# A 16-batch conv, attention and FFN kernel on one Trainium2 core: state blocks by head, z turned by DMA, other PSUM banks in the first phase

## The chip, the cores and the metric

The program runs on one core of one Trainium2 chip. The metric is the device time of one execution, in microseconds (us). Engines: PE (TensorE, the matrix engine; PEld are its weight loads), DVE (VectorE), ACT (ScalarE), POOL (GpSimd) and SP (SyncE, which here only issues DMAs; SPq is its DMA queue in the profile). Each engine runs its own instruction stream in order, and they meet only at semaphores.

## The reference, cut to what matters

x is 16 batches of 128 channels by 1024 positions. A channel mix by a 128x128 inverse gives t, 1024 tokens of 128 channels in each batch. Then

```python
t = t + attn(ln(t))          # causal linear attention, 8 heads of 16, feature map elu + 1
t = t + ffn(ln(t))           # gate averaged over the tokens picks W1, W2 of the batch
# attn: q, k, v = ln(t) @ W.T ; S = cumsum(k (x) v) ; z = cumsum(k)
#       out = (q @ S) / max(q . z, 1e-6) @ Wout.T
```

In the kernel most matrix operands are split into two f16 parts, hi and lo (lo = value - hi), and a product is made of two or three f16 matmuls.

## The kernel before

The first phase walks over 128 tiles (16 batches of 8 tiles of 128 tokens). For each tile the engines run named steps. TENSOR_ORDER, SCALAR_ORDER, VECTOR_ORDER, GPSIMD_ORDER and SYNC_ORDER give, for each engine, the steps in the order in which they are issued inside one **slot**, each with a skew: in slot s a step of skew k works on tile s - k. So one slot holds work on many tiles, and the time of the first phase is about 128 slots and a fill and a drain. The batches between the first and the last are a hardware loop with 8 slots in it; `batch` writes one batch out. Every step waits on semaphores for what it reads and for the buffer that it overwrites.

The steps, by tile: SP loads x; ACT `split_x` makes x_hi and POOL `split_x` makes x_lo (every second slot, two tiles at once); PE `conv` writes t into a bank of PSUM; DVE `stats1`, `mean_var1`, `eps1` and POOL `rsqrt1` (a power of one column) give 1/std; PE `project` writes q, k and v; ACT `exp_qk`, `relu_qk` and DVE `make_qk` (min(exp, 1) + relu) give q and k; `q_hi` (ACT), `k_hi` and `qk_lo` (POOL) split them into `qk_parts`; SP `turn` transposes that block by DMA into `qkT_parts`; ACT `v_hi` and DVE `v_lo` split v; PE `state` adds k (x) v to the running state in the bank `p_s`; PE `scores` writes a mask and k q into the banks `p_a`; ACT `scores_hi` and DVE `scores_lo` split them; PE `values` makes the numerators and denominators; DVE `denominator`, `invert`, `divide`; PE `turn_out`, ACT `copy_out`, PE `out_project` (which also adds the conv again), ACT `read_t1`; DVE `stats2`, `mean_var2`, `eps2`, POOL `rsqrt2`, DVE `normalise` give z = ln(t); z has to be turned and split for the gate (PE `gate`, ACT `gate_relu`) and for the second phase.

PSUM before: `p_in` has two banks (tiles of even and odd number), `p_a` one pair for the 1024 columns of the scores, `p_m1` one bank shared by `conv`, `out_project` and `gate`, `p_m2` one shared by `turn_out` and `turn_z`, and `p_o` and `p_s` one each. `bank_read` makes a step wait until the previous user of its bank has been read.

The state before is made for two heads at once, 128 rows of k parts by 2 x 17 columns, with 8 matmuls. The blocks across heads are of no use, so DVE `read_state` multiplies the bank by a mask into f32, and POOL `state_hi` and `state_lo` split it. z is turned by PE (`turn_z`) into `p_m2`, ACT `z_hi` and DVE `z_lo` split it from there.

Between the first batch and the loop SP sends the parts of the base FFN weights to memory and back (`base_parts`, then `W_hi_lo_rows`), and its later DMAs stand behind that.

The second phase (merged weights by batch, FFN, layer norm, store) begins when all gates are there and is not touched.

## Time and profile before

| | |
|---|---|
| median of 3 runs (lowest, highest) | 848.0 us (845.4, 848.01) |
| the profiled execution | 848.7 us |
| its span, first to last instruction | 846.9 us |
| busy share of the span: PE, PEld, DVE, ACT, POOL | 87%, 64%, 88%, 79%, 63% |
| mean granted PE clock, share of full speed | 0.969 |
| DMA | 74.10 MB, mean 87 GB/s |

Durations are those of the hardware profiler. Instructions of one engine overlap a little: the next one starts before the previous one's recorded end, so from one start to the next is often less than a duration. A matmul's recorded duration contains the way through the array and says little about how fast matmuls follow one another.

### The profile page before, as it was taken

The numbers are of one execution on the slowest core, as the hardware profiler recorded it, in microseconds if no ns is written. First come the engines' busy times: TensorE is split into PE (matmuls) and PEld (weight loads), VectorE is DVE, ScalarE is ACT, GpSimd is POOL, SyncE is SP. The second block draws the span as 40 slices with busy tenths as digits, with TensorE's granted clock in tenths as the row PEclk, the third lists the DMA queues.
The fourth block names the chain that finished last, engine by engine and source line by source line (L and its number), as shares of the span: only waits on it lengthen the run. The fifth ranks groups of instructions, "written<-read, shape, count | busy, mean of one in ns | idle before, by whom it ended". The sixth has DMA issues, their size and how long they took to land. (4 is left out here: it accounts for less than half of the span.)

```text
span 846.9 us, 37199 instructions
## 1 busy us (share of the span) xinstructions
PE 739.7 (87%) x11168; PEld 538.4 (64%) x11168; DVE 742.6 (88%) x2736; ACT 670.2 (79%) x1875; POOL 534.6 (63%) x1009
## 2 busy tenths in 40 slices
PE   1588999999999999999999999968899998899994
PEld 1255666666666666666666666648577777577773
DVE  6587999999999999999999999955788985689894
ACT  1477898999989989998898988844788885688884
POOL 5486888888888888888988988810133342033333
PEclk9888999999999999999999999977999999999998
DMA  2255444454444444544454444410022221122222
GB/s 80 52 126 118 98 111 105 92 117 109 91 111 106 105 105 100 116 106 99 106 111 95 116 100 98 88 33 26 2 77 86 77 74 51 38 64 76 74 87 75
DMA packets 165473, 74.10 MB, mean 87 GB/s; under 512 B 139212, under 2 KB 152687, under 8 KB 165368
## 3 DMA queue, kind: packets, MB, share of 16 engines
q1 hardware_dynamic: 165432, 73.58, 36.0%
q8 instruction: 23, 0.38, 0.2%
q14 instruction: 18, 0.15, 0.1%
HBM read 22.69 MB, written 17.30 MB: 47 GB/s over the span
## 5 line engine op out<-in xcount | busy, mean ns | idle before, releaser
L795 DVE SCALAR_TENSOR_TENSOR scores_lo<-p_a,scores_hi 128x512 f16<-128x512 f32 x256 | 164.0, 682 | 0.0
L698 ACT ACTIVATE scores_hi<-p_a 128x512 f16<-128x512 f32 x256 | 138.5, 600 | 6.4 <-PE p_a L543 6.2
L861 POOL TENSOR_TENSOR stats<-stats,consts 128x1 f32<-128x1 f32 x128 | 78.1, 610 | 75.7 <-DVE stats L745 75.6
L1312 POOL TENSOR_TENSOR ffn_rstd_shift<-ffn_rstd_shift,consts 128x4 f32<-128x4 f32 x32 | 36.7, 1146 | 132.8 <-DVE ffn_rstd_shift L1271 132.8
L886 POOL TENSOR_TENSOR qk_parts<-qk_f,qk_parts 128x128 f16<-128x128 f32 x256 | 104.9, 429 | 0.1
L867 POOL TENSOR_TENSOR stats<-stats,consts 128x1 f32<-128x1 f32 x128 | 89.0, 695 | 18.7 <-DVE stats L751 17.1
L560 PE MATMUL p_o<-v_parts,scores_hi 128*128 128x17 f16 x1024 | 90.2, 171 | 12.1 <-ACT scores_hi L698 6.2
L560 PEld LDWEIGHTS p_o<-v_parts,scores_hi 128*128 128x128 f16 x1024 | 80.4, 96 | 30.0 <-issue 27.6
L1095 PE MATMUL psb<-merged_W_of_batch,h_hi 128*128 128x128 f16 x512 | 94.2, 220 | 4.9 <-DVE h_lo L1249 3.8
L1249 DVE TENSOR_TENSOR h_lo<-h_f,h_hi 128x512 f16<-128x512 f32 x128 | 95.0, 782 | 1.2 <-ACT h_hi L1152 1.2
L1141 ACT ACTIVATE h_f<-psb,merged_b_of_batch 128x512 f32<-128x512 f32 x128 | 87.0, 711 | 11.4 <-PE psb L1076 11.3
L1097 PE MATMUL psb<-merged_W_of_batch,h_lo 128*128 128x128 f16 x512 | 93.8, 219 | 0.0
L1096 PE MATMUL psb<-merged_W_of_batch,h_hi 128*128 128x128 f16 x512 | 93.8, 219 | 0.0
L564 PE MATMUL p_o<-v_parts,scores_lo 128*128 128x17 f16 x1024 | 89.7, 170 | 0.0
L562 PE MATMUL p_o<-v_parts,scores_hi 128*128 128x16 f16 x1024 | 89.5, 170 | 0.0
L1161 ACT ACTIVATE normed<-psb,ffn_rstd_shift 128x128 f32<-128x128 f32 x128 | 48.1, 456 | 41.6 <-DVE ffn_rstd_shift L1277 41.6
L562 PEld LDWEIGHTS p_o<-v_parts,scores_hi 128*128 128x128 f16 x1024 | 80.3, 96 | 0.3 <-issue 0.2
L564 PEld LDWEIGHTS p_o<-v_parts,scores_lo 128*128 128x128 f16 x1024 | 80.0, 96 | 0.0
L768 DVE SCALAR_TENSOR_TENSOR qk_f<-exp_qk,relu_qk 128x256 f32<-128x256 f32 x128 | 75.3, 589 | 4.7 <-ACT exp_qk L666 3.4
L536 PE MATMUL p_a<-mask_bf,ident_bf 128*128 128x512 bf16 x256 | 78.1, 386 | 0.4 <-DVE scores_lo L795 0.4
L1305 POOL TENSOR_TENSOR normed<-normed,ln_gain_rows 128x512 f32<-128x512 f32 x32 | 40.7, 1272 | 58.5 <-ACT normed L1161 58.5
L650 ACT ACTIVATE t<-p_m 128x128 f32<-128x128 f32 x128 | 35.5, 277 | 47.7 <-PE p_m L589 45.5
(195 smaller groups left out, 3009.6 us busy)
## 6 DMA issues: line engine op xcount, KB each, us to landing
x_f<-in_x SPq DMA_DIRECT2D x32, 256.0 KB, 2.9
t_rows<-t SPq DMA_DIRECT2D x64, 128.0 KB, 1.9
t_back<-t_rows SPq DMA_DIRECT2D x32, 256.0 KB, 2.6
out<-out_tile SPq DMA_DIRECT2D x32, 256.0 KB, 2.0
tv_share<-in_L_ffn_tv_W SPq DMA_DIRECT2D x32, 128.0 KB, 2.2
qkT_parts<-qk_parts SPq DMA_TRANSPOSE x128, 3.1
...
```

Source lines behind the costliest of these rows:

```text
L560: mm(num[:, h, :], hi, vp[:, t, h, 0:VW], start=(h == 0), stop=False, skip_group_check=True)
L562: mm(num[:, h, 0:DH], hi, vp[:, t, h, VW:VW + DH], start=False, stop=False, skip_group_check=True)
L564: last = mm(num[:, h, :], lo, vp[:, t, h, 0:VW], start=False, stop=True, skip_group_check=True)
L698: nc.scalar.activation(ah[:, t % 2, cols], p_a[:, cols], ACT.Relu).then_inc(ahi_ready[eo], 1)
L795: nc.vector.scalar_tensor_tensor(al[:, t % 2, cols], p_a[:, cols], 0.0, ah[:, t % 2, cols], ALU.max, ALU.subtract).then_inc(alo_ready[eo], 1)
L867: nc.gpsimd.tensor_tensor(s[:, 8:9], s[:, 9:10], mhalf, ALU.pow).then_inc(rstd2, 1)
L886: last = nc.gpsimd.tensor_tensor(lo, src, pk[:, t % 4, w, :, 0:DH], ALU.subtract)
L1095: mm(o, hi, w2b[:, bb, 0, c, :], start=False, stop=False)
L1096: mm(o, hi, w2b[:, bb, 1, c, :], start=False, stop=False)
L1097: last = mm(o, lo, w2b[:, bb, 0, c, :], start=False, stop=(c == FC - 1))
L1141: nc.scalar.activation(hf_[:, c, :], ps[:, c, :], ACT.Relu, bias=b1s[:, h // 2, c:c + 1], scale=1.0 / WS).then_inc(h_ready[c], 1)
L1249: nc.vector.tensor_tensor(hl[:, h % 2, c, :], hf_[:, c, :], hh[:, h % 2, c, :], ALU.subtract)\
```

## The change

- **State by head.** PE `state` makes 16 matmuls of 64 weight columns by 17 or 16, each head into its own 64 partitions of `p_s`. DVE clears `p_s` once at the start, so that the blocks across heads stay zero. `read_state`, its f32 tile and the multiplication by ones are gone: ACT `state_hi` and DVE `state_lo` split the bank directly.
- **z by DMA.** `turn_z` on PE is gone. ACT `z_hi` and POOL `z_lo` split z before it is turned, and SP `turn_z` transposes both parts with one DMA into `zT_hi_lo`.
- **Banks.** `p_in` has one bank; `p_a` has two pairs; `conv`, `out_project`, `turn_out` and `gate` share `p_m1`.
- **Engines and order.** `q_hi` goes from ACT to POOL. All order tables and skews are other ones; the deepest skew is 12 where it was 8, so two batches are written out on either side of the loop.

```diff
-TENSOR_ORDER = [("conv", 0), ("project", 0), ("turn_out", 5), ("gate", 8), ("values", 4), ("turn_z", 7),
-                ("state", 2), ("out_project", 5), ("scores", 2)]
+TENSOR_ORDER = [("scores", 3), ("out_project", 6), ("values", 4), ("conv", 0), ("state", 2), ("turn_out", 5),
+                ("project", 0), ("gate", 11)]
...
-GPSIMD_ORDER = [("qk_lo", 2), ("state_lo", 4), ("split_x", 0), ("rsqrt2", 7), ("state_hi", 3), ("k_hi", 1),
-                ("rsqrt1", 0)]
-SYNC_ORDER = [("turn", 2), ("load_x", 3), ("load_tv", 3), ("store", 7)]
+GPSIMD_ORDER = [("rsqrt1", 1), ("rsqrt2", 8), ("split_x", 0), ("z_lo", 9), ("k_hi", 1), ("q_hi", 1), ("qk_lo", 1)]
+SYNC_ORDER = [("turn_z", 9), ("load_x", 3), ("load_tv", 3), ("store", 7), ("turn", 1)]
...
-            p_in = pa_.enter_context(nc.psum_tensor("p_in", [P, 2, 512], F32))
+            p_in = pa_.enter_context(nc.psum_tensor("p_in", [P, 512], F32))
...
-            p_a = pa_.enter_context(nc.psum_tensor("p_a", [P, NH * P], F32))
+            p_a = pa_.enter_context(nc.psum_tensor("p_a", [P, 2, NH * P], F32))
...
-            p_m2 = pa_.enter_context(nc.psum_tensor("p_m2", [P, 512], F32))
...
+                    def turn_z(b, t):
+                        n = TILES * b + t
+                        parts = n + 1 if isinstance(n, int) else sp.to_reg(n + 1)
+                        sp.wait_ge(ones_set, 1)
+                        sp.wait_ge(zlo_ready, parts)
+                        sp.dma_start_transpose(zz[:, :, bass.ds(n * P, P)],
+                                               zp[:, t % 4, :, :].rearrange("p w c -> p (w c)"))\
+                            .then_inc(z_turned[t % 4], 16)
...
-                    banks = [{"conv": (bn1,), "out_project": (t1_ready,), "gate": (gate_ready,)},
-                             {"turn_out": (oT_ready,), "turn_z": (zhi_ready, zlo_ready)}]
+                    banks = [{"conv": (bn1,), "out_project": (t1_ready,), "turn_out": (oT_ready,),
+                              "gate": (gate_ready,)}]
...
-                        at_least(pe, exp_ready, n - 1)
-                        at_least(pe, relu_ready, n - 1)
-                        at_least(pe, vlo_ready, n - 1)
+                        at_least(pe, exp_ready, n)
+                        at_least(pe, relu_ready, n)
+                        at_least(pe, vlo_ready, n)
...
-                        for a in range(NP):
-                            kk = pk[:, t % 4, 1, 2 * a:2 * a + 2, :].rearrange("p h c -> p (h c)")
-                            mm(sbank[:, a, :], kk, vp[:, t, 2 * a:2 * a + 2, 0:VW],
-                               start=(t == 0 and a == 0), stop=False, skip_group_check=True)
...
+                        for h in range(NH):
+                            e, kk = h % 2, pk[:, t % 4, 1, h, :]
+                            o = sbank[64 * e:64 * e + 64, h // 2, e * VW:(e + 1) * VW]
+                            mm(o, kk, vp[:, t, h, 0:VW], start=(t == 0 and h < 2), stop=False, skip_group_check=True)
...
-                            at_least(pe, ahi_ready[eo], n)
-                            at_least(pe, alo_ready[eo], n)
-                            mm(p_a[:, eo * 512:(eo + 1) * 512], identb[:, :],
+                            at_least(pe, ahi_ready[eo], n - 1)
+                            at_least(pe, alo_ready[eo], n - 1)
+                            mm(p_a[:, t % 2, eo * 512:(eo + 1) * 512], identb[:, :],
...
+                    def state_hi(b, t):
+                        if t == TILES - 1:
+                            return
+                        m = (TILES - 1) * b + t
+                        act.wait_ge(su_done, m + 1)
+                        at_least(act, av_done, TILES * b + t - 2)
+                        nc.scalar.activation(sp2[:, t % 4, 0, :, :], sbank, ACT.Copy).then_inc(sh_ready, 1)
...
+                        nc.vector.tensor_tensor(sp2[:, t % 4, 1, :, :], sbank, sp2[:, t % 4, 0, :, :], ALU.subtract)\
+                            .then_inc(sp_ready, 1)
...
-                    def z_lo(b, t):
-                        n = TILES * b + t
-                        dve.wait_ge(zhi_ready, n + 1)
-                        cols = bass.ds(n * P, P)
-                        nc.vector.tensor_tensor(zl[:, cols], p_m2[:, P:2 * P], zh[:, cols], ALU.subtract)\
-                            .then_inc(zlo_ready, 1)
...
+                    def z_lo(b, t):
+                        n = TILES * b + t
+                        pool.wait_ge(zhi_ready, n + 1)
+                        nc.gpsimd.tensor_tensor(zp[:, t % 4, 1, :], z_[:, t % 2, :], zp[:, t % 4, 0, :], ALU.subtract)\
+                            .then_inc(zlo_ready, 1)
```

What the tables make of the engines' streams is shown at three places. First POOL in a slot of the loop in which x is split. Before, from `rsqrt1` on (L861; L886 is `qk_lo`, L902 `state_lo`, L911 `split_x`, L867 `rsqrt2`, L895 `state_hi`, L877 `k_hi`):

```order
L861 TENSOR_TENSOR stats<-stats,consts 128x1 [waits ve1]
L886 TENSOR_TENSOR qk_parts<-qk_f,qk_parts 128x8x16 [waits khi_ready,qhi_ready]
L886 TENSOR_TENSOR qk_parts<-qk_f,qk_parts 128x8x16
L902 TENSOR_TENSOR state_parts<-state_f,state_parts 128x136 [waits sh_ready]
L910 REGISTER_ALU
L911 TENSOR_TENSOR x_lo<-x_f,x_hi 128x256 [waits xh_ready]
L866 REGISTER_ALU
L867 TENSOR_TENSOR stats<-stats,consts 128x1 [waits ve2]
L893 REGISTER_ALU
L895 TENSOR_TENSOR state_parts<-state_f,state_ones 128x136 [waits av_done,sm_ready]
L877 CAST qk_parts<-qk_f 128x8x32 [waits av_done,qk_ready,ones_set]
```

In the change, the same kind of slot (L855 `rsqrt1`, L861 `rsqrt2`, L900 `split_x`, L891 `z_lo`, L875 `k_hi` and then `q_hi`, L885 `qk_lo`):

```order
L855 TENSOR_TENSOR stats<-stats,consts 128x1 [waits ve1]
L860 REGISTER_ALU
L861 TENSOR_TENSOR stats<-stats,consts 128x1 [waits ve2]
L899 REGISTER_ALU
L900 TENSOR_TENSOR x_lo<-x_f,x_hi 128x256 [waits xh_ready]
L891 TENSOR_TENSOR z_parts<-z,z_parts 128x128 [waits zhi_ready]
L867 REGISTER_ALU
L875 CAST qk_parts<-qk_f 128x8x32 [waits sc_done_0,sc_done_1,qk_ready,ones_set]
L875 CAST qk_parts<-qk_f 128x16x16 [waits sc_done_0,sc_done_1,qk_ready,ones_set]
L885 TENSOR_TENSOR qk_parts<-qk_f,qk_parts 128x8x16 [waits khi_ready,qhi_ready]
L885 TENSOR_TENSOR qk_parts<-qk_f,qk_parts 128x8x16
```

The two state steps are gone, `z_lo` and `q_hi` have come, and `k_hi`, `q_hi` and `qk_lo` of a tile now follow `rsqrt1` of the same tile in one slot, with `rsqrt2` ahead of them.

Second DVE in the loop. Before, from `make_qk` (L768) through `divide` (L814), `v_lo` (L759), `z_lo` (L833) and the statistics to `normalise` (L776):

```order
L768 SCALAR_TENSOR_TENSOR qk_f<-exp_qk,relu_qk 128x256 [waits lo_ready,relu_ready,exp_ready]
L814 TENSOR_TENSOR attn_out<-p_o,denominators 128x128 [waits ot_done,den2]
L759 SCALAR_TENSOR_TENSOR v_parts<-p_in,stats,v_parts 128x8x16 [waits relu_ready,exp_ready,vhi_ready]
L833 ISA [waits zhi_ready]
L833 TENSOR_TENSOR zT_lo<-p_m,zT_hi 128x128
L725 REGISTER_ALU
L726 BN_STATS stats<-p_m 128x6 [waits conv_done]
L821 BN_STATS stats<-t 128x6 [waits t1_ready]
L732 BN_AGGR stats<-stats 128x2 [waits bn1,ones_set]
L827 BN_AGGR stats<-stats 128x2 [waits bn2,ones_set]
L745 TENSOR_SCALAR stats<-stats 128x1 [waits mv1]
L776 TENSOR_SCALAR z<-t,stats 128x128 [waits zt_done,rstd2,mv2]
```

In the change a slot begins with `normalise` (L778) and `make_qk` (L770), then `state_lo` (L786) and `v_lo` (L761):

```order
L778 TENSOR_SCALAR z<-t,stats 128x128 [waits zlo_ready,rstd2,mv2]
L770 SCALAR_TENSOR_TENSOR qk_f<-exp_qk,relu_qk 128x256 [waits lo_ready,relu_ready,exp_ready]
L785 REGISTER_ALU
L786 TENSOR_TENSOR state_parts<-p_s,state_parts 128x136 [waits sh_ready]
L761 SCALAR_TENSOR_TENSOR v_parts<-p_in,stats,v_parts 128x8x16 [waits relu_ready,exp_ready,vhi_ready]
L726 REGISTER_ALU
L727 BN_STATS stats<-p_m 128x6 [waits conv_done]
L828 BN_AGGR stats<-stats 128x2 [waits bn2,ones_set]
L734 BN_AGGR stats<-stats 128x2 [waits bn1,ones_set]
L802 TENSOR_SCALAR denominators<-p_o 128x8 [waits av_done]
L747 TENSOR_SCALAR stats<-stats 128x1 [waits mv1]
L808 RECIPROCAL denominators<-denominators 128x8 [waits den1]
```

`z_lo` with its wait for ACT is gone, `normalise`, which waits for `rsqrt2`, now stands directly ahead of `make_qk`, and `make_qk` works on the tile whose 1/std POOL gave in the same slot.

Third PE around the state stage. Before (L569 is the end of `values`, L595 `turn_z`, L524 and L526 `state`, of which four pairs follow one another):

```order
L569 MATMUL p_o<-state_parts,qkT_parts 128x34 x8
L595 MATMUL p_m<-consts,z 128x128 [waits oT_ready,z_ready]
L362 REGISTER_ALU [waits vlo_ready,vhi_ready,khi_ready,lo_ready]
L524 MATMUL p_s<-v_parts,qk_parts 128x34 [waits sm_ready]
L526 MATMUL p_s<-v_parts,qk_parts 128x2x16
```

In the change (L531 and L535 are `state`, L585 `turn_out`, L513 the first matmul of `project`):

```order
L531 MATMUL p_s<-v_parts,qk_parts 64x17 [waits sp_ready]
L531 MATMUL p_s<-v_parts,qk_parts 64x17 x7
L535 MATMUL p_s<-v_parts,qk_parts 64x16 x8
L489 REGISTER_ALU [waits o_ready]
L585 MATMUL p_m<-consts,attn_out 128x128 [waits bn1]
L358 REGISTER_ALU
L513 MATMUL p_in<-w_in_hi,x_hi 128x384 [waits vlo_ready,relu_ready,exp_ready]
```

Eight matmuls of 128 output partitions are now sixteen of 64, `turn_z` has left PE, and `turn_out` and `project` stand behind the state with waits for DVE (bn1, vlo_ready).

## Rows read from the trace of the kernel before

**Rows 1.** Busy time in two windows: span, PE, PEld, DVE, ACT, POOL, clock, DMA share, GB/s.
```profile
...
200.00:300.00 100.00, 91.69 (x1568) 64.22 (x1566) 97.86 (x396) 90.22 (x288) 85.50 (x179) 1.00 0.47 106
540.00:560.00 20.00, 17.30 (x325) 12.61 (x325) 18.20 (x72) 14.57 (x50) 12.17 (x27) 0.99 0.36 80
```

**Rows 2.** Groups by line, 200 to 500 us: busy us, mean ns | idle before.
```profile
...
L886 POOL TENSOR_TENSOR qk_parts<-qk_f,qk_parts 128x128 f16<-128x128 f32 x148 | 60.7, 429 | 0.0
...
L867 POOL TENSOR_TENSOR stats<-stats,consts 128x1 f32<-128x1 f32 x74 | 51.7, 699 | 3.9 <-DVE stats L751 2.7
...
L861 POOL TENSOR_TENSOR stats<-stats,consts 128x1 f32<-128x1 f32 x74 | 45.4, 614 | 39.5 <-DVE stats L745 39.5
L768 DVE SCALAR_TENSOR_TENSOR qk_f<-exp_qk,relu_qk 128x256 f32<-128x256 f32 x75 | 45.1, 601 | 0.8
...
L689 ACT ACTIVATE qk_parts<-qk_f 128x256 f16<-128x256 f32 x74 | 31.3, 423 | 2.2 <-DVE qk_f L768 2.2
L895 POOL TENSOR_TENSOR state_parts<-state_f,state_ones 128x136 f16<-128x136 f32 x64 | 30.0, 468 | 0.0
...
L877 POOL CAST qk_parts<-qk_f 128x256 f16<-128x256 f32 x74 | 29.1, 393 | 0.0
L902 POOL TENSOR_TENSOR state_parts<-state_f,state_parts 128x136 f16<-128x136 f32 x65 | 28.5, 439 | 0.0
...
L776 DVE TENSOR_SCALAR z<-t,stats 128x128 f32<-128x128 f32 x74 | 25.6, 346 | 0.5
```

**Rows 3.** Waits, 200 to 500 us: total us, times, longest us.
```profile
...
POOL stats L861 <- DVE stats L745: 39.5, 74, 1.1
```

**Rows 4.** Timeline of DVE: start us, us, instruction, from one batch to the next.
```profile
...
291.37 0.68 DVE L739 SCALAR_TENSOR_TENSOR tv_lo<-tv_share,tv_hi 128x512 f32 x1
...
298.57 0.27 DVE L833 TENSOR_TENSOR zT_lo<-p_m,zT_hi 128x128 f32 x1
298.77 0.28 DVE L726 BATCH_NORM_STATS2 stats<-p_m 128x6 f32<-128x128 f32 x1
...
323.72 0.69 DVE L739 SCALAR_TENSOR_TENSOR tv_lo<-tv_share,tv_hi 128x512 f32 x1
```

**Rows 5.** Timeline of POOL, same columns, 305 to 310 us.
```profile
...
305.35 0.66 POOL L911 TENSOR_TENSOR x_lo<-x_f,x_hi 128x256 f16<-128x256 f32 x1
305.98 0.72 POOL L867 TENSOR_TENSOR stats<-stats,consts 128x1 f32<-128x1 f32 x1
...
309.52 0.80 POOL L867 TENSOR_TENSOR stats<-stats,consts 128x1 f32<-128x1 f32 x1
```

**Rows 6.** Timeline of DVE, same columns, 305 to 310 us.
```profile
...
305.46 0.83 DVE L768 SCALAR_TENSOR_TENSOR qk_f<-exp_qk,relu_qk 128x256 f32<-128x256 f32 x1
...
309.54 0.37 DVE L768 SCALAR_TENSOR_TENSOR qk_f<-exp_qk,relu_qk 128x256 f32<-128x256 f32 x1
```

**Rows 7.** Timeline of PE around the state stage, from 300.5 us.
```profile
...
300.58 0.31 PE L595 MATMUL p_m<-consts,z 128*128 128x128 f32 x1
...
300.72 0.18 PE L524 MATMUL p_s<-v_parts,qk_parts 128*128 128x34 f16 x1
...
300.93 0.22 PE L585 MATMUL p_m<-w_in_hi,x_hi 128*128 128x128 f16 x1
...
300.98 0.22 PE L586 MATMUL p_m<-w_in_lo,x_hi 128*128 128x128 f16 x1
```

**Rows 8.** Timeline of SP's DMA queue, 54 to 72 us.
```profile
...
55.17 0.47 SPq L446 DMA_DIRECT2D base_parts<-base_ffn_lo  x1
59.27 2.76 SPq L452 DMA_DIRECT2D W_hi_lo_rows<-base_parts  x4
62.31 1.34 SPq L401 DMA_TRANSPOSE qkT_parts<-qk_parts  x1
```

**Rows 9.** Waits, 56 to 72 us, columns as in the waits above.
```profile
...
PEld p_a L543 <- DMA qkT_parts<-qk_parts: 4.9, 1, 4.9
```

**Rows 10.** DMA issues: queue, kind, count, median us to landing.
```profile
...
qkT_parts<-qk_parts SPq DMA_TRANSPOSE x128, 3.1
```

More of the change, by code:

```diff
@@ L454, in _ @@
                                 .then_inc(base_placed, 16)
-                    with sp.Fori(1, B - 1) as b:
+                    batch(stages, 1)
+                    with sp.Fori(2, B - 1) as b:
                         batch(stages, b)
-                    batch(no_loads, B - 1)
-                    batch(no_loads, B, new=False)
+                    for b in range(B - 1, B + 2):
+                        batch(stages, b)
                     for pair in range(TILES // 2):
@@ L608, in _ @@
                     pe.wait_ge(ones_set, 1)
+                    pe.wait_ge(state_cleared, 1)
                     run(pe, TENSOR_ORDER, {"conv": conv, "project": project, "state": state,
-                        "scores": scores, "values": values, "turn_out": turn_out, "out_project": out_project, "turn_z": turn_z,
+                        "scores": scores, "values": values, "turn_out": turn_out, "out_project": out_project,
                         "gate": gate})
@@ L914, in _ @@
                     run(pool, GPSIMD_ORDER, {"rsqrt1": rsqrt1, "qk_lo": qk_lo,
-                        "state_hi": state_hi, "state_lo": state_lo, "split_x": split_x,
-                        "rsqrt2": rsqrt2, "k_hi": k_hi})
+                        "split_x": split_x,
+                        "rsqrt2": rsqrt2, "q_hi": qk_hi(0, qhi_ready), "k_hi": qk_hi(1, khi_ready), "z_lo": z_lo})
         with ExitStack() as pb:
```

201 lines of the change are left out of this document (88 added, 113 removed).

## The prediction

> **What bounds the kernel now.** Only the first phase is touched, and the windows of busy time [rows 1], which I read first, say who sets its rate. In 100 us of the loop DVE is busy 97.86 us, PE 91.69, ACT 90.22 and POOL 85.50, at full clock; DVE has almost nothing left. The length of a tile's slot comes from an instruction that DVE runs once a batch, the split of the FFN share: 291.37 to 323.72 us is 32.35 us for 8 slots [rows 4], so 4.04 us a slot. DVE's share is 0.979 x 4.04 = 3.96 us, POOL's 3.45, ACT's 3.64. The table of waits shows POOL waiting for DVE 74 times for 39.5 us in 300 [rows 3]: 0.53 us in every slot, with POOL late only because DVE is. So DVE is the bound, and a step taken off DVE shortens the slot until POOL, PE or a loop between them takes over.
>
> One property of DVE's and POOL's work decides how much is left. `make_qk` lasts 0.37 us when it meets a short POOL instruction [rows 6], but 0.83 us when it meets `split_x`: it starts at 305.46 and ends at 306.29, 0.28 us after `split_x` ended (305.35 + 0.66 = 306.01) [rows 5, 6]. POOL pays as well: `rsqrt2` beside `make_qk` takes 0.80 us at 309.52 and 0.72 at 305.98 [rows 5]. The two are kept apart where both read SBUF with two inputs. On average `make_qk` takes 0.601 us [rows 2], so DVE loses 0.23 us a slot to this.
>
> **The change part by part, for one slot.**
>
> DVE: `z_lo` goes. It costs the 0.20 us from its start to the next one's (298.57 to 298.77) [rows 4]. `read_state` becomes `state_lo`, the same shape from the same bank: nothing either way. DVE is then at 3.96 - 0.20 = 3.76 us with the collisions of today and 3.53 without any.
>
> POOL: `state_hi` and `state_lo` go, 7 in 8 slots: (0.468 + 0.439) x 7/8 = 0.79. `q_hi` comes at the price of `k_hi`, 0.39, and `z_lo` at that of one `qk_lo` of the same 128 columns, 0.43 [rows 2]. Together +0.03: 3.48 us.
>
> ACT: `q_hi` (0.42) goes [rows 2], `state_hi` comes; the trace has no ACT step of its width from PSUM, but between nothing and the 0.42 of a 256 column one ACT stays at or under 3.64. I take it as no bound.
>
> PE: `turn_z` goes, 0.14 us (300.58 to 300.72). The state stage took 0.21 us for 8 matmuls (300.72 to 300.93), 0.026 each. No row shows a matmul with 64 weight columns. Sixteen at 0.026 are 0.42; at 0.05, the spacing of matmuls with 128 columns of data (300.93 to 300.98), 0.80 [rows 7]. The data are 17 columns or fewer, which is nearer to the first, so I take 0.42, with 0.80 kept for the range. With 0.42 PE goes from 3.71 busy to 3.78, and being pipelined it is less loaded than that says. Here a page speaks against the change: the Trainium skill, TensorE Tiling, section Restrictions, says that column tiling, which is what a 64 column output block is, turns off the fast weight load. The sum by it is worked out as a rival below from rows.
>
> The loop between POOL and DVE is new, and I take it as what binds next. In one slot POOL does `rsqrt1`, `rsqrt2`; DVE `normalise` waits for `rsqrt2`, and `make_qk` is queued behind it; POOL's `k_hi`, `q_hi`, `qk_lo` wait for `make_qk`; and the next slot's `rsqrt1` stands behind them on POOL. With durations from [rows 2], [rows 5] and [rows 6], and 0.55 for `rsqrt2` (its 0.699 less about 0.15 of collision; the undisturbed one is bounded by `rsqrt1`'s 0.614):
> - a slot without `split_x`: 0.61 + 0.55 + `normalise` 0.35 + `make_qk` 0.37 + 0.39 + 0.39 + 2 x 0.43 = 3.52; `z_lo` fits beside DVE's two.
> - a slot with it: 0.61 + 0.55 + 0.66 + 0.28 (`make_qk` past `split_x`) + `z_lo` 0.43 + 0.39 + 0.39 + 0.86 = 4.17.
>
> The mean is 3.85. ACT's `exp_qk` and `relu_qk` need only `rsqrt1`, so they run beside `rsqrt2` and `normalise`. DVE's own 3.76 has to fit into the same slots, and there are semaphore delays; I take **3.88 us**, 0.16 less than now.
>
> The single bank of `p_in` makes `project` wait for `v_lo` of the tile just before. It is fourth on DVE, and `project` is next to last on PE, behind values and state; I put it at nothing, and if `v_lo` came later each 0.1 us would be 0.1 us of slot. The one bank for four users adds a ring (`gate`, `gate_relu`, `out_project`, `read_t1`, `conv`, `stats1`, `turn_out`, `copy_out`); between the PE members other PE steps stand that cover the readers, and the second pair of score banks takes away the wait of the mask matmuls for `scores_lo`. I put these two against each other at nothing.
>
> SP: the turn of q and k is issued one slot skew earlier and used one later. After the first batch SP holds the weight parts (55.17, then 59.27 for 2.76 us) and the next turn is issued only at 62.31 [rows 8]; PE waits 4.9 us for it [rows 9]. Two slots, about 8 us, now lie between a turn and its scores, so I take back 4 of the 4.9. In the loop a turn lands in 3.1 us [rows 10], inside those two slots. The turn of z is a quarter as large; two slots lie before its gate too.
>
> Drain: the last tile's z goes by DMA, at most 3.1 us [rows 10], in place of one short PE step: +3 us. The fall of DVE's busy share after 540 us [rows 1] says that the loop's rate ends near 548; from 70 us that is 478 / 4.04 = 118 slots.
>
> Sum, against the profiled execution's own 848.7 us (span 846.9): 118 x 0.16 = -18.9; weight parts -4; drain +3. That is 828.8. The median of the runs is 0.7 lower than this execution: **828 us**.
>
> **The rivals.**
> - *DVE stays the bound* (0.17). The collisions are gone or no worse, and the slot is 3.6 to 3.76: 118 x 0.28 = 33 less at 3.76, 815 us; 803 at 3.66. For it: DVE's sum is the largest today. Against it: `make_qk` now starts just when POOL is at `split_x` or `z_lo`.
> - *The collisions eat the gain* (0.17). If `make_qk` and `normalise` meet a POOL instruction in every slot, the slot without `split_x` grows by `z_lo`'s 0.43 as well: 3.95 and 4.17, mean 4.06, today's 4.04 in all but name. Time: 848 + 2 - 4 + 3 = 849; at 4.00 it is 842.
> - *State by head is slow* (0.13), the case on the other side. The stage stands on PE ahead of `turn_out` and `project`, for which DVE and ACT wait. PE has 4.04 - 3.71 = 0.33 idle and gets 0.14 back, so from a stage of 0.21 + 0.33 + 0.14 = 0.68 us on it decides. At 0.80 the slot is 4.16: +14 us, 848 + 14 - 4 + 3 = 861. This is what the page's rule would do: losing the fast load on half as many columns. [...] No row here tells.
> - *A DMA is late* (0.05). SP issues `turn_z` ahead of `turn`, a turn's issue takes 1.34 us of the queue [rows 8], and the loads of x share the engines. If one turn in four lands 1 us late that is 0.25 a slot, which cancels the gain: 845 to 860.
>
> **How the numbers follow.** The forecast (slot 3.80 to 3.97, 820 to 839 us) gets 0.48. The ends leave out about 1 in 10 each: low 806, where DVE alone would bound, high 857, between the late DMA and a state stage of 0.80 us. A difference under 0.3% can't be told from none here. Faster holds the forecast, the first rival, and less than half of the second, with a little of the two last: 0.76. Same is 0.07, slower 0.17.
>
> **What would show it.** Slot of 3.88 us between two FFN splits of DVE, in pairs of a short and a long slot; DVE busy about 95%; POOL over 90% busy and no longer waiting for `eps1` but for `make_qk`; DVE idle before `normalise` on `rsqrt2`; `make_qk` still well above 0.37 us on average; state stage 0.42 us; no 4.9 us wait for the turn after the first batch. It is wrong if PE's `turn_out` or `project` have idle time before them in every slot, if DVE waits for `conv`, or if the scores wait for a turn.

## The result, and the profile after

The changed kernel takes 864.27 us (median of 4 runs, 861.35 to 866.63) where the kernel before takes 847.61 beside it: ratio 1.02, 95% interval 1.0164 to 1.0237. It is slower, by 16.7 us; forecast were 828 us and a range that ends at 857. The profiled executions differ by 17.9 us of span (846.9 and 864.8), and DVE's FFN splits say where these went. First the changed kernel, then the one before: the fourth and the last of the 16 splits on DVE, and the last `gate_relu` on ACT, which ends the first phase (columns: start us, us).

```profile
136.85 0.68 DVE L741 SCALAR_TENSOR_TENSOR tv_lo<-tv_share,tv_hi 128x512 f32 x1
...
530.73 0.68 DVE L741 SCALAR_TENSOR_TENSOR tv_lo<-tv_share,tv_hi 128x512 f32 x1
...
588.12 0.19 ACT L714 ACTIVATION_READ_ACCUMULATOR gate_hidden<-p_m,gate_b 128x1 f32 x1
```

```profile
129.65 0.69 DVE L739 SCALAR_TENSOR_TENSOR tv_lo<-tv_share,tv_hi 128x512 f32 x1
...
517.80 0.68 DVE L739 SCALAR_TENSOR_TENSOR tv_lo<-tv_share,tv_hi 128x512 f32 x1
...
570.46 0.19 ACT L713 ACTIVATION_READ_ACCUMULATOR gate_hidden<-p_m,gate_b 128x1 f32 x1
```

- **Start-up:** the fourth split is 7.2 us later.
- **Loop:** 12 batches take 393.88 us instead of 388.15: +5.7, a slot of 4.10 us instead of 4.04 (forecast 3.88).
- **Drain:** from the last split to the last gate 57.4 us instead of 52.7: +4.7.
- What is left, 0.3 us, is the second phase.

So the loop, which should have given 15 us in these 96 slots (0.16 each), costs 6. The windows of the changed kernel, to be held against [rows 1]: the granted clock is 0.79 between 60 and 100 us (0.91 before), and DVE has work in 95.83% of a slot, so 0.958 x 4.10 = 3.93 us (3.76 forecast, 3.96 before).

```profile
60.00:100.00 40.00, 32.11 (x508) 22.01 (x506) 28.84 (x110) 25.52 (x81) 24.85 (x56) 0.79 0.69 113
200.00:300.00 100.00, 94.42 (x1698) 65.01 (x1699) 95.83 (x364) 85.92 (x282) 81.75 (x183) 1.00 0.55 121
```

The groups by line, 200 to 500 us, answer to [rows 2]. `make_qk` came down (601 to 504 ns), but `normalise`, which was never disturbed, went up from 346 to 492; POOL now waits for `make_qk` (44.0 us ahead of L875; the trace names no releaser, but `k_hi` starts 0.11 to 0.13 us after the end of `make_qk` in every slot between 296 and 400 us) where it waited for `eps1`.

```profile
L770 DVE SCALAR_TENSOR_TENSOR qk_f<-exp_qk,relu_qk 128x256 f32<-128x256 f32 x73 | 36.8, 504 | 7.3 <-ACT relu_qk L675 5.1
L778 DVE TENSOR_SCALAR z<-t,stats 128x128 f32<-128x128 f32 x73 | 35.9, 492 | 1.5
...
L875 POOL CAST qk_parts<-qk_f 128x256 f16<-128x256 f32 x146 | 54.0, 398 | 44.0 <-issue 44.0
L855 POOL TENSOR_TENSOR stats<-stats,consts 128x1 f32<-128x1 f32 x73 | 40.1, 549 | 0.9
```

The waits of the same stretch (total us, times, longest) name two places that the prediction had put at nothing: ACT's `gate_relu` waits for PE's `gate`, and PE's `turn_out` for DVE's `stats1`.

```profile
ACT gate_hidden L714 <- PE p_m L606: 23.9, 54, 0.6
...
PEld p_m L585 <- DVE stats L727: 10.8, 19, 0.6
PE p_m L585 <- DVE stats L727: 8.3, 19, 0.5
```

They belong to one ring. Timelines of the changed kernel, DVE, then PE, then ACT:

```profile
304.67 0.43 DVE L770 SCALAR_TENSOR_TENSOR qk_f<-exp_qk,relu_qk 128x256 f32<-128x256 f32 x1 [0.23 <-ACT relu_qk L675]
...
305.22 0.35 DVE L761 SCALAR_TENSOR_TENSOR v_parts<-p_in,stats,v_parts 128x128 f16<-128x128 f32 x1
305.55 0.30 DVE L727 BATCH_NORM_STATS2 stats<-p_m 128x6 f32<-128x128 f32 x1
...
307.99 0.62 DVE L778 TENSOR_SCALAR z<-t,stats 128x128 f32<-128x128 f32 x1
308.55 0.65 DVE L770 SCALAR_TENSOR_TENSOR qk_f<-exp_qk,relu_qk 128x256 f32<-128x256 f32 x1
```

```profile
305.90 0.33 PE L585 MATMUL p_m<-consts,attn_out 128*128 128x128 f32 x1 [0.39 <-DVE stats L727]
306.10 0.32 PE L513 MATMUL p_in<-w_in_hi,x_hi 128*128 128x384 f16 x1
...
306.70 0.23 PE L604 MATMUL p_m<-zT_hi_lo,gate_hi 128*128 x1
...
306.82 0.23 PE L606 MATMUL p_m<-zT_hi_lo,gate_hi 128*128 x1
```

```profile
306.27 0.28 ACT L682 ACTIVATE attn_outT<-p_m 128x128 f32<-128x128 f32 x1
...
307.17 0.37 ACT L714 ACTIVATE gate_hidden<-p_m,gate_b 128x128 f32<-128x128 f32 x1
...
307.53 0.47 ACT L667 ACTIVATE exp_qk<-p_in,stats 128x256 f32<-128x256 f32 x1
307.88 0.47 ACT L675 ACTIVATE relu_qk<-p_in,stats 128x256 f32<-128x256 f32 x1
```

The reader is to see a circle. `stats1` ends at 305.85 and `turn_out` starts 0.05 us later, though it needs nothing from it: it writes into the bank that `stats1` reads. `project` and `gate` are queued behind `turn_out`, and by the code `gate` also waits until `copy_out` has read the shared bank (`copy_out` ends at 306.55, `gate` starts at 306.70); `gate_relu` waits for `gate`; `exp_qk` and `relu_qk` stand behind it; `make_qk` needs them, and in the first slot shown it waits 0.23 us for `relu_qk`; `v_lo` and the next `stats1` stand behind `make_qk`. The next turn is at 309.45 and 309.79, again 0.05 after its end, and in the ten slots from 268 to 306 us `turn_out` always starts 0.05 to 0.07 after the end of `stats1`.

The circle does not hold every step of every slot. At 308.55 `make_qk` stands behind `normalise`, while `relu_qk` had ended at 308.35. There a second loop closes, the one between POOL and DVE of the prediction. POOL's timeline (L875 is `k_hi` and `q_hi`, L855 `rsqrt1`, L861 `rsqrt2`):

```profile
305.21 0.74 POOL L875 CAST qk_parts<-qk_f 128x256 f16<-128x256 f32 x2 [0.85 <-issue]
...
306.81 0.55 POOL L855 TENSOR_TENSOR stats<-stats,consts 128x1 f32<-128x1 f32 x1
307.34 0.55 POOL L861 TENSOR_TENSOR stats<-stats,consts 128x1 f32<-128x1 f32 x1
...
309.32 0.74 POOL L875 CAST qk_parts<-qk_f 128x256 f16<-128x256 f32 x2 [0.41 <-issue]
```

`rsqrt2` ends at 307.89 and `normalise` starts 0.10 later; `make_qk` ends at 309.20 and `k_hi` starts 0.12 later. Between 296 and 400 us `normalise` starts 0.09 to 0.20 us after `rsqrt2` in every slot.

### The profile page after: what moved, and what is told of

Its sections match the earlier page's. It is cut to its first block and busy times, and to the rows that moved or that the text cites. A ratio compares the mean times of both kernels' runs of the same rounds, so it can differ in the third digit from the quotient of the medians.

```text
span 864.8 us, 38688 instructions
## 1 busy us (share of the span) xinstructions
PE 759.3 (88%) x11936; PEld 545.2 (63%) x11936; DVE 734.9 (85%) x2609; ACT 652.8 (75%) x1859; POOL 519.5 (60%) x1040
## 5 line engine op out<-in xcount | busy, mean ns | idle before, releaser
L795 DVE SCALAR_TENSOR_TENSOR scores_lo<-p_a,scores_hi 128x512 f16<-128x512 f32 x256 | 169.5, 663 | 0.0
L875 POOL CAST qk_parts<-qk_f 128x256 f16<-128x256 f32 x256 | 95.5, 402 | 83.3 <-issue 78.5
L885 POOL TENSOR_TENSOR qk_parts<-qk_f,qk_parts 128x128 f16<-128x128 f32 x256 | 108.1, 443 | 10.3
L569 PE MATMUL p_o<-v_parts,scores_hi 128*128 128x16 f16 x1024 | 89.5, 170 | 0.0
L567 PEld LDWEIGHTS p_o<-v_parts,scores_hi 128*128 128x128 f16 x1024 | 83.1, 96 | 1.2 <-issue 1.2
L714 ACT ACTIVATE gate_hidden<-p_m,gate_b 128x128 f32<-128x128 f32 x128 | 46.9, 367 | 48.2 <-PE p_m L606 46.3
L770 DVE SCALAR_TENSOR_TENSOR qk_f<-exp_qk,relu_qk 128x256 f32<-128x256 f32 x128 | 64.0, 500 | 21.8 <-ACT relu_qk L675 17.0
L569 PEld LDWEIGHTS p_o<-v_parts,scores_hi 128*128 128x128 f16 x1024 | 80.4, 96 | 1.5
L861 POOL TENSOR_TENSOR stats<-stats,consts 128x1 f32<-128x1 f32 x128 | 70.2, 549 | 17.5 <-DVE stats L753 16.7
L855 POOL TENSOR_TENSOR stats<-stats,consts 128x1 f32<-128x1 f32 x128 | 70.3, 549 | 13.2 <-DVE stats L747 11.9
```

What stands on the lines that cost most here:

```text
L567: mm(num[:, h, :], hi, vp[:, t, h, 0:VW], start=(h == 0), stop=False, skip_group_check=True)
L569: mm(num[:, h, 0:DH], hi, vp[:, t, h, VW:VW + DH], start=False, stop=False, skip_group_check=True)
L795: nc.vector.scalar_tensor_tensor(al[:, t % 2, cols], p_a[:, t % 2, cols], 0.0, ah[:, t % 2, cols], ALU.max, ALU.subtract).then_inc(alo_rea ...
L875: nc.gpsimd.tensor_copy(dst, src.unsqueeze(2).broadcast_to([P, NH, 2, DH])).then_inc(done, 1)
L885: last = nc.gpsimd.tensor_tensor(lo, src, pk[:, t % 4, w, :, 0:DH], ALU.subtract)
```

## The experiments

All are times of the whole program, with the kernel before on the same chip at 847.2 to 847.7 us. Slot is the distance of two FFN splits in mid-loop divided by 8; z and qk are the mean durations of `normalise` and `make_qk`.

| kernel | us | ratio, 95% interval | slot us | z, qk ns |
|---|---|---|---|---|
| ring | 902.2 | 1.0649 (1.0618 to 1.0681) | 4.46 | 493, 429 |
| zlast | 877.6 | 1.0347 (1.033 to 1.0364) | 4.25 | 475, 418 |
| turnbank | 851.35 | 1.006 (1.0037 to 1.0083) | 4.025 | 491, 541 |
| gatebank | 860.53 | 1.016 (1.0134 to 1.0187) | 4.06 (two of 12 batches 4.2) | 490, 528 |
| gatelate | 858.75 | 1.0134 (1.0111 to 1.0157) | 4.07 (two of 12 batches 4.2) | 490, 541 |
| detour | 862.25 | 1.0173 (1.0152 to 1.0194) | 4.11 | 494, 514 |
| tb_norm | 864.8 | 1.0193 (1.0167 to 1.0219) | 4.11 | 365, 551 |
| tb_detour | 849.63 | 1.003 (1.0017 to 1.0043) | 4.025 | 494, 543 |
| stateonly | 908.61 | 1.0718 (1.0701 to 1.0736) | 4.53 | 346, 428 |
| stateonly2 | 863.65 | 1.0175 (1.0152 to 1.0198) | 4.16 | 346, 474 |
| oldbanks | 873.56 | 1.031 (1.0279 to 1.0342) | 4.26 | 346, 425 |
| oldbanks2 | 838.27 | 0.9896 (0.988 to 0.9913) | 3.91 | 347, 454 |
| ob_detour | 835.28 | 0.9853 (0.9822 to 0.9883) | 3.91 | 346, 455 |
| ob_vlo | 831.63 | 0.9801 (0.9781 to 0.9821) | 3.865 | 353, 479 |
| onebank | 948.9 | 1.1122 (1.1046 to 1.1197) | 4.66 to 5.4 | 347, 424 |
| best | 830.1 | 0.9795 (0.9778 to 0.9812) | 3.86 | 352, 478 |

### The first four: two orders, and the parts of the change apart

**ring** and **zlast** are the changed kernel with other orders, against the ring and against the collisions.

```diff
 # ring
-... ("turn_out", 5), ("project", 0), ("gate", 11)]
+... ("gate", 11), ("project", 0), ("turn_out", 5)]
 # SCALAR_ORDER: gate_relu (skew 11) and copy_out (5) at the end
 # zlast
-GPSIMD_ORDER = [..., ("split_x", 0), ("z_lo", 9), ("k_hi", 1), ("q_hi", 1), ("qk_lo", 1)]
+GPSIMD_ORDER = [..., ("split_x", 0), ("k_hi", 1), ("q_hi", 1), ("qk_lo", 1), ("z_lo", 9)]
 # SYNC_ORDER: turn ahead of turn_z
```

> The changed kernel with three steps moved: gate stands before project on TensorE, turn_out after it, and gate_relu comes from near the head of ScalarE's slot to its end, before copy_out. Theory R (the ring of the one bank: statistics of conv, turn_out, copy_out, gate, gate_relu, and behind gate_relu exp, relu, make_qk, v_lo and the next statistics): gate_relu no longer stands ahead of exp, a slot falls from 4.10 to about 3.9 us, 840 to 845 us. Theory C (collisions of DVE and POOL set the slot): exp comes earlier, nothing else, slot within 0.03 of 4.10, 861 to 866 us. Theory D (DMA of z and turns late): no change either.

> The changed kernel with z_lo at the end of POOL's slot instead of ahead of k_hi, and the turn of z after the turn of q and k on the queue. Theory C: normalise and make_qk no longer meet z_lo, normalise falls from 0.49 to near 0.35 us in half of the slots and make_qk from 0.50 to about 0.45, slot down by 0.15, about 845 us. Theory R: the ring holds make_qk only through exp and relu; gain under 0.05 a slot, 858 to 864 us.

Both missed. In ring ACT's `copy_out` waits for PE 31.4 us in 300 and DVE's `make_qk` for `relu_qk` 29.0: the new order made new waits, and the run says nothing on the old ones. In zlast `make_qk` did come down to 418 ns, but DVE now waits 24.9 us in 300 ahead of `normalise`. What it waits for is `rsqrt2`: between 296 and 400 us `normalise` starts 0.08 to 0.20 us after its end in every slot. Here it ends at 331.09:

```profile
330.54 0.55 POOL L861 TENSOR_TENSOR stats<-stats,consts 128x1 f32<-128x1 f32 x1
```

```profile
331.19 0.35 DVE L778 TENSOR_SCALAR z<-t,stats 128x128 f32<-128x128 f32 x1 [0.39 <-issue]
```

`z_lo` now stands on POOL between `qk_lo` and `rsqrt1`, so that every lap of the loop between POOL and DVE contains it. With this loop longer (SP's order changed too) the slot went from 4.10 to 4.25. A collision taken away is no gain if a wait replaces it.

**oldbanks** has state by head, z by DMA and q_hi on POOL, with the banks of before and nearly its order. **stateonly** is the kernel before with state by head alone.

```diff
 # oldbanks (stateonly keeps q_hi, z_lo, turn_z as before)
+TENSOR_ORDER = [("conv", 0), ("project", 0), ("turn_out", 5), ("gate", 10), ("values", 4), ("state", 2),
+                ("out_project", 5), ("scores", 2)]
+SCALAR_ORDER = [("split_x", 0), ("state_hi", 3), ("relu_qk", 1), ("exp_qk", 1), ("read_t1", 6), ...]
+VECTOR_ORDER = [("denominator", 5), ("state_lo", 3), ("invert", 5), ("make_qk", 1), ...]
+GPSIMD_ORDER = [("qk_lo", 2), ("split_x", 0), ("rsqrt2", 7), ("z_lo", 8), ("k_hi", 1), ("q_hi", 1), ("rsqrt1", 0)]
```

> State by head, z turned by DMA and q_hi on POOL as in the change, but the banks of before (two for q k v, one pair for scores, turn_out in a bank of its own) and the order and skews of before for what was there. My sum without the new loops: DVE at 3.76 us a slot, so 3.8 to 3.9, 825 to 835 us. Theory R says this, since the one bank and the new order are gone. Theories C and D, which blame the work moved to POOL and to the DMA queue, say 848 us or more.

> The kernel before with state by head alone: state_hi on ScalarE, state_lo on DVE in the place of read_state, both state steps off POOL, all else as before. DVE still has z_lo and stays the bound: slot 4.04, 846 to 849 us, down to 842 if fewer collisions with POOL count. If sixteen matmuls of 64 columns cost over 0.68 us a slot it is slower, 855 or more; the changed kernel's trace has the stage at about 0.3 us, which says no.

Both missed their sums (825 to 835 and 846 to 849 us). The waits of stateonly show why: ACT waits for PE's state stage, 44.0 us in 300 (30.8 in oldbanks), ahead of `relu_qk` and `exp_qk`, and so for something that the tile's q and k don't need. That was where I had put `state_hi`.

```profile
ACT state_parts L705 <- PE p_s L525: 44.0, 58, 1.0
```

### Cutting the ring in the changed kernel

The second bank of the upper half of the scores is given up, since `scores_lo_1` is done when the next mask matmuls start. The freed bank goes to `turn_out` (**turnbank**), or to `gate` (**gatebank**); **gatelate** is gatebank with `gate_relu` behind `relu_qk`.

```diff
-            p_a = pa_.enter_context(nc.psum_tensor("p_a", [P, 2, NH * P], F32))
+            p_a = pa_.enter_context(nc.psum_tensor("p_a", [P, 3, 512], F32))   # bank 2 if eo else t % 2
+            p_m2 = pa_.enter_context(nc.psum_tensor("p_m2", [P, 512], F32))
 # turnbank; in gatebank and gatelate the gate stands alone
-                    banks = [{"conv": (bn1,), "out_project": (t1_ready,), "turn_out": (oT_ready,),
-                              "gate": (gate_ready,)}]
+                    banks = [{"conv": (bn1,), "out_project": (t1_ready,), "gate": (gate_ready,)},
+                             {"turn_out": (oT_ready,)}]
```

> The changed kernel with one edit on its banks: the second bank of the upper half of the scores is given up, and turn_out gets that bank for itself; every order stays. Theory R (a ring through the one bank sets the slot: gate, gate_relu, exp_qk, relu_qk, make_qk, v_lo, stats1, turn_out, project, gate; in the trace of the changed kernel gate_relu is at 303.29, 307.17 and 311.14 us, make_qk at 304.67, stats1 at 305.55 and turn_out at 305.90, with 0.39 us of idle before it released by stats1): the ring is cut between stats1 and turn_out, PE no longer waits for stats1 (10.8 + 8.3 us in 300 now), gate comes up to 0.39 us earlier, ACT's wait of 23.9 us before gate_relu shrinks below 10, slot 4.10 to about 3.95, time 845 to 852. Theory C (DVE's own work with the collisions is the bound, 3.93 us a slot busy): PE's wait moves elsewhere, the slot stays within 0.04 of 4.10, time 860 to 866. If the single upper score bank itself costs, scores wait for scores_lo_1 and the time is above 868.

> As turnbank, but the freed bank goes to gate and turn_out stays in the shared one. Theory R: the ring does not go through the wait of out_project for gate_relu, nor gate's for copy_out, so nothing changes: 860 to 868. It is the control for the single upper score bank (scores wait for scores_lo_1, which ends at 307.01 where the mask matmuls start at 306.95) and the base for gatelate. Theory C says the same.

> gatebank with one more edit: gate_relu stands behind relu_qk on ACT instead of ahead of exp_qk. Theory R: the ring is cut between gate and exp_qk; exp_qk no longer waits for PE's gate (23.9 us in 300, 0.32 a slot), make_qk comes 0.3 to 0.8 us earlier against rsqrt1, POOL's wait for make_qk (44.0 us in 300) shrinks to 30 or less; slot to 3.95, 845 to 852. Theory C: within 4 us of gatebank.

turnbank came as the ring's theory said in time, though its slot of 4.025 is not the 3.95 expected: 12.9 us under the changed kernel, with one bank moved and no order touched. Its `turn_out` starts at 303.65, ahead of the end of `stats1` (303.42 + 0.29 = 303.71), and no wait for `stats1` is left among its large ones. DVE is now full again:

```profile
200.00:300.00 100.00, 92.84 (x1733) 66.32 (x1733) 97.99 (x372) 87.02 (x285) 83.27 (x187) 1.00 0.56 122
```

gatebank is 3.7 us under the changed kernel, inside the range expected for no change, and the two intervals overlap. Its `gate` no longer waits for `copy_out`: it starts 0.16 to 0.17 us after `project`'s last matmul in nine of the ten slots from 268 to 306 us, where the changed kernel has 0.19 to 0.40.

gatelate missed (its slot at 4.07, not 3.95), and corrects the theory. ACT no longer waits for `gate` ahead of `exp_qk`, but then waits there for `rsqrt1`: in nine slots from 270 to 305 us `exp_qk` starts 0.03 to 0.12 after the end of `rsqrt1`, and 0.20 to 0.85 after `project`. So the ring went through the gate. PE still waits for `stats1`, but what holds `exp_qk` is now POOL, in the other loop.

```profile
ACT exp_qk L671 <- POOL stats L859: 29.9, 61, 0.9
...
PEld p_m L589 <- DVE stats L731: 15.9, 29, 0.8
PE p_m L589 <- DVE stats L731: 11.4, 20, 0.8
```

From one `k_hi` to the next, over the eight slots of a batch, the last one with the FFN split (us, read from the timelines of POOL between 296 and 400 us):

| kernel | laps | sum |
|---|---|---|
| changed | 4.11, 3.83, 4.08, 3.84, 4.14, 3.84, 4.14, 4.83 | 32.81 |
| turnbank | 4.25, 3.82, 4.09, 3.65, 4.21, 3.64, 4.21, 4.33 | 32.20 |
| gatelate | 4.36, 3.84, 4.09, 3.66, 4.20, 3.66, 4.20, 4.51 | 32.52 |

The ring costs the changed kernel 0.2 us in two short laps and 0.5 in the lap with the FFN split, and the long laps give some of it back. Six of gatelate's laps are turnbank's within 0.02. It loses in the other two; there `turn_out` waits 0.74 us for `stats1`, which stands on DVE behind the split, and how that reaches the loop no run isolates.

**tb_norm** is turnbank with `normalise` behind `stats1` on DVE.

> turnbank with one more edit: normalise stands behind stats1 on DVE instead of first, so that make_qk is no longer queued behind it and z is made while POOL casts k_hi and q_hi instead of while it runs split_x. Theory C (what is left over 3.76 us a slot is DVE kept off SBUF by POOL: z 491 ns on average against 346 before, 620 beside split_x at 301.97 us): z falls to 400 or less, DVE's busy time per slot falls by 0.1, slot 4.025 to 3.93, time 838 to 844. Rival: the casts k_hi and q_hi hold DVE off just as split_x does, or rsqrt2 now stands in the loop in another place; z stays at 450 ns or more and the time within 3 us of turnbank's 851.

z fell to 365 ns, so it is the meeting with `split_x` that lengthens it (in the changed kernel 0.62 beside `split_x`, 0.38 in the slots without). The time missed: 865 us, outside both expectations. The 3.77 us of DVE work that followed did not become the slot. DVE waits for `v_hi` (12.2 us) and PE's masks for `scores_lo` (25.7 us): the collision was bought off with waits once more.

### The parts of the change with the old banks

**oldbanks2** and **stateonly2** are oldbanks and stateonly with two steps moved.

```diff
-SCALAR_ORDER = [("split_x", 0), ("state_hi", 3), ("relu_qk", 1), ("exp_qk", 1), ("read_t1", 6), ...]
-VECTOR_ORDER = [("denominator", 5), ("state_lo", 3), ("invert", 5), ("make_qk", 1), ("divide", 5), ...]
+SCALAR_ORDER = [("split_x", 0), ("relu_qk", 1), ("exp_qk", 1), ("state_hi", 3), ("read_t1", 6), ...]
+VECTOR_ORDER = [("denominator", 5), ("invert", 5), ("make_qk", 1), ("divide", 5), ("state_lo", 3), ...]
```

> The kernel before with state by head alone, as stateonly, but with state_hi on ACT between exp_qk and read_t1 (where ACT has 0.41 us idle, 301.22 to 301.63, in the kernel before) and state_lo on DVE behind divide. Theory P (the +61 us of stateonly came from state_hi ahead of relu_qk and exp_qk on ACT, so that ACT waited for PE's state stage 44 us in 300): DVE is the bound again, 843 to 853. Rival: state by head costs by itself (state_lo has to wait for ACT, PE's stage is longer), and it stays above 865.

> State by head, z by DMA and q_hi on POOL with the banks and nearly the order of the kernel before, as oldbanks, but with state_hi between exp_qk and read_t1 on ACT and state_lo behind divide on DVE. DVE has lost z_lo (0.20) and, with z not first, meets split_x with make_qk alone: DVE busy 3.76 a slot. If the new banks and order are what the change lost by, this is 825 to 840. If it is a loop between POOL and DVE (rsqrt1, k_hi, q_hi, qk_lo behind make_qk), the slot is 3.95 to 4.05 and the time 843 to 852.

The places of these two steps alone were worth 45 us (stateonly) and 35 us (oldbanks). oldbanks2 beats the kernel before by 9 us. It does the same work per tile as the changed kernel, which the new banks, order and skews thus make 26 us slower, and its windows give DVE 0.954 x 3.91 = 3.73 us a slot.

```profile
200.00:300.00 100.00, 93.91 (x1810) 68.58 (x1810) 95.39 (x382) 91.61 (x296) 86.57 (x192) 1.00 0.57 125
```

State by head alone does not pay (+16 us, outside both expectations). It moves work from POOL, which waits 87.6 us in 300 for `eps1` in stateonly2, to ACT; what sets its slot of 4.16 no run isolates. oldbanks2 has z by DMA and `q_hi` on POOL besides and is 25 us faster; the two were not taken apart.

**onebank** is oldbanks2 with one edit, turn_out in the shared bank; **ob_vlo** is oldbanks2 with `v_lo` ahead of `state_lo`.

```diff
 # onebank
-                    banks = [{"conv": (bn1,), "out_project": (t1_ready,), "gate": (gate_ready,)},
-                             {"turn_out": (oT_ready,)}]
+                    banks = [{"conv": (bn1,), "out_project": (t1_ready,), "turn_out": (oT_ready,),
+                              "gate": (gate_ready,)}]
 # ob_vlo
-VECTOR_ORDER = [..., ("divide", 5), ("state_lo", 3), ("v_lo", 2), ...]
+VECTOR_ORDER = [..., ("divide", 5), ("v_lo", 2), ("state_lo", 3), ...]
```

> oldbanks2 with one edit: turn_out goes into the bank that conv, out_project and gate share, as in the changed kernel; all orders stay. The prediction put the one bank for four users at nothing (with the second pair of score banks against it). Theory R: each matmul of the bank waits for the reader of the one before: turn_out for stats1 (about 0.3 us behind), and gate, which stands right behind turn_out, for copy_out on ACT, which comes behind scores_hi (0.3 to 0.5 us): slot 3.91 to 4.2 or more, 865 or more. The prediction's own claim: within 4 us of 838.

> oldbanks2 with state_lo behind v_lo on DVE instead of ahead of it. project waits for v_lo (PEld 21.9 and PE 12.6 us in 300 us ahead of p_in). If project's wait is in the loop that sets 3.91 us a slot, v_lo 0.20 us earlier gives up to 0.08 a slot: 829 to 835. Rival: the wait is only PE running ahead, and the slot stays 3.91: 837 to 840.

onebank costs 111 us. In mid-loop its slot is 4.66 at full clock, and longer in other batches; between 200 and 300 us the granted clock is 0.90 (1.00 in oldbanks2), so a part of the 111 us is the clock's. The timeline of PE and the waits show it: `gate` follows `turn_out` by 0.90 us (0.10 in oldbanks2, 301.23 to 301.33), because `copy_out` on ACT must first read the other 128 columns of the bank.

```profile
320.26 0.30 PE L581 MATMUL p_m<-consts,attn_out 128*128 128x128 f32 x1
321.16 0.23 PE L600 MATMUL p_m<-zT_hi_lo,gate_hi 128*128 x1 [0.60 <-ACT attn_outT L678]
```

```profile
ACT gate_hidden L710 <- PE p_m L602: 45.8, 61, 0.9
PE p_m L600 <- ACT attn_outT L678: 36.2, 61, 0.7
```

ob_vlo gains 6.6 us over oldbanks2: `project`'s wait for `v_lo` was in the loop (PE's part of it falls from 12.6 to 4.4 us in 300), and DVE is at 96.96% of a slot of 3.865.

### The start-up

After batch 0 SP's queue holds the weight parts. In the changed kernel:

```profile
60.64 1.72 SPq L457 DMA_DIRECT2D W_hi_lo_rows<-base_parts  x4
...
62.93 1.34 SPq L399 DMA_TRANSPOSE qkT_parts<-qk_parts  x1
64.36 2.60 SPq L408 DMA_TRANSPOSE zT_hi_lo<-z_parts  x1
```

```profile
PEld p_a L550 <- DMA qkT_parts<-qk_parts: 5.7, 1, 5.7
...
PE p_a L550 <- DMA qkT_parts<-qk_parts: 5.2, 1, 5.2
```

```profile
68.00:76.00 8.00, 6.52 (x82) 4.50 (x83) 3.76 (x15) 3.10 (x9) 1.87 (x5) 0.50 0.54 96
```

PE waits 5.2 us for a turn, up to 69.48, and in each 2 us from 66 to 76 its granted clock is 0.50, the lower level of 1.2 GHz. From 90 to 96 it is 0.50 again, behind a wait of 1.6 us for another turn. Before, the wait was 4.4 us up to 65.97, and the clock was 0.50 from 66 to 70 (0.70 in the 2 us ahead, 0.59 in the 2 us behind). **detour**, **tb_detour**, **ob_detour** and **best** (from ob_vlo) put these transfers behind the last batch of SP's queue.

```diff
                     batch(stages, 0)
-                    ... base_parts out, W_hi_lo_rows in ...
                     batch(stages, 1)
 ...
+                    ... base_parts out, W_hi_lo_rows in ...
                     for pair in range(TILES // 2):
```

> The changed kernel with the detour of the weight parts (base_parts out, W rows in: six transfers between batch 0 and batch 1 of SP's queue) put behind the last batch of that queue. Theory S (the +7 us up to batch 4 are turns issued late behind the detour, then the clock at half speed): start of batch 4's tv_lo moves from 136.85 to 130 to 133, and the time falls by 4 to 7 minus what the transfers now cost ahead of the second phase (0 to 4): 857 to 864. Rival: the start-up is lost for another reason (two batches of prologue, a slower drain of the turns of z), and batch 4 stays at 135 or later.

> turnbank with the detour of the weight parts behind the last batch of SP's queue, as in the kernel detour. If the start-up stall and the ring add up independently, batch 4's tv_lo falls from 134.03 to about 126 and the time from 851 to 843 (839 to 847). If what is gained at the start is lost at the end of the phase (detour gained 8 us in one profiled execution but 2 in the median), it is 848 to 850.

> oldbanks2 (838.3 us) with the detour of the weight parts behind the last batch of SP's queue. In oldbanks2 the second batch takes 37.76 us (59.03 to 96.79) where later ones take 31.29. Theory S (the detour holds the turns back there): the second batch falls to 32 to 34, batch 4's tv_lo from 129.24 to 124 to 126, and the time to 833 to 836. Rival (the loads and stores lost at the start are paid at the end of the phase, as tb_detour's 1.7 us of gain for 5.9 us of earlier batch 4 suggest): 837 to 840.

> ob_vlo (831.6 us) with the detour of the weight parts behind the last batch of SP's queue. In ob_vlo the second batch takes 38.68 us where later ones take 30.92. If the two edits add up as ob_detour (3.0 us less than oldbanks2) and ob_vlo (6.6 less) did apart: 828 to 830. If they don't, the start-up gain is lost at the end of the phase: 831 to 833.

detour, tb_detour and ob_detour came in the ranges of their expectations (tb_detour in that of its second reading); best lies between its two. In the profiled execution of detour the fourth split starts at 127.64 us, 9.2 earlier, and the span is 8.3 shorter, but that execution is the fastest of its kernel and the changed kernel's is the slowest of its own. The medians of the four pairs differ by only 2.0, 1.7, 3.0 and 1.5 us. In the profiled executions the last gate comes 8.8, 6.1, 4.0 and 3.0 us earlier, and what follows it is 0.5, 5.0, 1.2 and 3.5 us longer. The four W transfers now stand ahead of the second phase's first load, which SP issues 3.5 us after the start of the last `gate_relu` instead of 1.6; what else lengthens that phase I can't place. best and ob_vlo ran in different sets, and their intervals overlap.

## Why the prediction was wrong

**"The one bank for four users adds a ring ... I put these two against each other at nothing."** This step failed. The ring was named, but priced by whether PE had other steps between the users of the bank, and the arm that closes it was not in it. What counts is where each reader stands in its own engine's order: `stats1` stands on DVE behind `make_qk`, which needs `relu_qk`; this stands on ACT behind `gate_relu`, which needs `gate`, and `gate` is on PE behind `turn_out`. In the changed kernel this costs 4.103 - 4.025 = 0.078 us a slot and 12.9 us in all (turnbank, although its PE now waits 10.0 us in 300 for `scores_lo` ahead of the masks). With another order the same sharing costs 111 us.

**"DVE is then at 3.76 us with the collisions of today."** This failed too, and by more. The work was priced rightly: oldbanks2, with the old banks and near the old order, has 3.73. The collisions were not those of today. `normalise` now stands first on DVE, just when POOL runs `split_x`, and takes 0.49 on average instead of 0.35. With `make_qk` at 0.541 against 0.454 of oldbanks2, turnbank has 0.144 + 0.087 = 0.23 us a slot more, and its DVE 3.95 against 3.73: the sizes agree. Without its ring the changed order still has a slot of 4.025, with DVE busy for 98% of it and the loop with POOL closed in every slot; no run separates the two. The time is close to that of the rival that the collisions eat the gain (4.06; 849 us; turnbank 851), but by luck: that rival had both steps disturbed in every slot, and in turnbank's short laps `normalise` takes 0.38 and `make_qk` 0.43.

**The loop over POOL, 3.52 and 4.17.** It is real: zlast made it longer, and the slot followed. turnbank's laps, the FFN split's pair aside, are 3.64 to 3.82 without `split_x` and 4.09 to 4.21 with it, 3.94 on average where the sums give 3.85. In a short one (`k_hi` at 286.88 and 290.53) POOL's steps up to the end of `rsqrt2` take 2.65 where 2.80 was summed, the two DVE steps 0.78 where 0.72 was, and the handovers to DVE and back, 0.10 and 0.12, stood at nothing. The sums also left out the FFN split. Beside it two `qk_lo` take 1.15 us instead of 0.81 and `rsqrt2` waits 0.44 for `eps2` (changed kernel), and the pair of laps that holds it is 8.58 us in turnbank where the other pairs are 7.85 to 7.91: 0.09 a slot. 3.85 + 0.09 + 0.09 is the 4.03 of turnbank.

**"I take back 4 of the 4.9."** Wrong: PE's weight loads wait 5.7 us where before they waited 4.9 [rows 9], and the clock stays low for 10 us; the fourth split is 7.2 us late instead of 4 early. Two slots of slack do not help when the queue is blocked for the whole detour, and `turn_z`, with 2.60 us of issue, is a further entry ahead of the next turn. detour shows that the place of these six transfers is the cause of the late fourth split.

**Drain +3:** 4.7 us from the last split to the last gate, a small miss. **`p_in` at nothing:** no wait of `project` for `v_lo` is among the changed kernel's large ones, so it held there.

**State by head is slow:** refuted. The timeline of PE has the 16 matmuls in about 0.30 us and the next step 0.46 after the first, where 0.42 was taken and 0.68 needed; that step, `turn_out`, waits for `stats1`, and in turnbank, where it doesn't, it follows by 0.35 (283.02 to 283.37).

```profile
309.33 0.30 PE L531 MATMUL p_s<-v_parts,qk_parts 128*64 128x17 f16 x8
309.48 0.28 PE L535 MATMUL p_s<-v_parts,qk_parts 128*64 128x16 f16 x8
309.79 0.33 PE L585 MATMUL p_m<-consts,attn_out 128*128 128x128 f32 x1
```

Eight of them are 0.15 us apart, 0.019 each against 0.026 before [rows 7]. The page that spoke against it, the Trainium skill's TensorEngine Tiling (Array Packing), section Gotcha 2: Feature Incompatibilities, says that column tiling excludes the fast weight load; the trace shows no cost of it at this size, and does not tell which way these weights were loaded.

Together, on the profiled executions: the twelve batches are 0.22 us a slot above the forecast, 21 us in 96 slots, of which the ring is 7.5. The fourth split is 7.2 us late where 4 and 15 slots of 0.16 early were forecast, 14 us. The drain and the second phase are 3. That is the 38 us by which the span of 864.8 misses the forecast 827.0 (846.9 - 19.9).
